# A two-layer state-space and attention kernel on one core: work moved across the seams between its stages

## The reference, cut to what matters

```
x = x + mixer(layernorm(x))        # state-space layer: 32 heads of 8 channels, 32 states
x = x + ffn0(layernorm(x))         # silu(w1 x) * (w2 x), gelu(h1 .), gelu(h2 .), w3
x = x + attention(layernorm(x))    # rms norm, 16 heads of 64, causal softmax, head gates, Wout
x = x + ffn1(layernorm(x))
```

## Time and profile before

| | |
|---|---|
| median of 3 runs | 1357.38 us (1356.96 to 1359.4) |
| profiled execution, own time | 1357.57 us |
| its span, first to last instruction | 1355.8 us |
| mean granted TensorE clock | 0.976 of full |
| busy: TensorE (PE) | 1277.2 us, 94% |
| busy: VectorE (DVE) | 908.5 us, 67% |
| busy: ScalarE (ACT) | 638.1 us, 47% |
| busy: GpSimd (POOL) | 588.2 us, 43% |
| moved by DMA | 143.51 MB, mean 106 GB/s |

### The profile page before, as it was taken

One profiled execution on the slowest core, in us unless ns is written; L12 is line 12 of the kernel. 1 busy time (PEld: TensorE's weight loads), 2 busy tenths in 40 slices (PEclk: granted clock), 3 DMA queues, 4 the chain that ended last, 5 costly groups with the idle time before them and its releaser, 6 DMA issues. The chain is left out here.

```text
span 1355.8 us, 22860 instructions
## 1 busy us (share of the span) xinstructions
PE 1277.2 (94%) x7798; PEld 709.1 (52%) x7798; DVE 908.5 (67%) x1773; ACT 638.1 (47%) x1537; POOL 588.2 (43%) x939
## 2 busy tenths in 40 slices
PE   7999677999999999998899998999999999899999
PEld 4443224566566566555445454555555556454545
DVE  6999996888988998989301206788787787530100
ACT  3266213555555565565322315566565665622221
POOL 2632315787888878888200002444344353410000
PEclk7999888999999999999899999999999999899999
DMA  2368896555555555556100002000000000000000
GB/s 81 155 256 339 317 391 218 192 183 183 187 188 184 183 185 190 185 183 235 63 0 0 0 1 88 1 1 1 1 1 1 1 1 1 1 1 0 16 0 15
DMA packets 67714, 143.51 MB, mean 106 GB/s; under 512 B 6800, under 2 KB 22800, under 8 KB 64784
## 3 DMA queue, kind: packets, MB, share of 16 engines
q1 hardware_dynamic: 62992, 129.47, 27.0%
q10 hardware_dynamic: 4608, 12.58, 2.3%
HBM read 94.58 MB, written 47.45 MB: 105 GB/s over the span
## 5 line engine op out<-in xcount | busy, mean ns | idle before, releaser
L1775 POOL TENSOR_SCALAR pr<-pr,rs,sg 128x512 f32<-128x512 f32 (+3 forms) x256 | 151.8, 607 | 209.4 <-DVE rs L1677 209.4
L615 PE MATMUL banks<-w_bc,valueT 128*128 128x512 f32 x448 | 212.0, 597 | 3.9 <-ACT own L909 3.1
L974 DVE TENSOR_TENSOR pp<-banks,rec 128x1024 f32<-128x1024 f32 x128 | 156.1, 1220 | 9.4 <-DMA dd<-det 3.3
L1588 ACT ACTIVATE pr<-banks,nm 128x512 f32<-128x512 f32 (+3 forms) x256 | 132.5, 523 | 24.9 <-DVE nm L1671 22.1
L615 PEld LDWEIGHTS banks<-w_bc,valueT 128*128 128x128 f32 x448 | 77.3, 192 | 61.4 <-issue 60.4
L1671 DVE TENSOR_REDUCE nm<-banks 128x2 f32<-128x1024 f32 (+3 forms) x128 | 105.5, 824 | 4.4
L1576 ACT COPY prT<-banks 128x512 f32<-128x512 f32 (+3 forms) x128 | 54.2, 424 | 112.0 <-PE banks L1472 111.8
L1056 POOL TENSOR_SCALAR_AFFINE_SELECT bp<-bp 128x1024 f32<-128x1024 f32 x64 | 73.5, 1148 | 76.4 <-ACT bp L863 76.3
L1312 DVE TENSOR_TENSOR x<-x,banks 128x256 f32<-128x256 f32 x16 | 6.7, 421 | 148.3 <-PE banks L1223 148.3
L856 ACT COPY qk<-banks 128x512 f32<-128x512 f32 x128 | 74.9, 585 | 64.2 <-PE banks L743 64.2
L1472 PE MATMUL banks<-ident,pr 128*128 128x128 f32 x640 | 98.7, 285 | 5.3 <-ACT prT L1576 4.1
(11 more groups left out here) (239 smaller groups left out, 2422.2 us busy)
## 6 DMA issues: line engine op xcount, KB each, us to landing
rec<-psi SPq DMA_DIRECT2D x128, 512.0 KB, 4.4
psi<-X SPq DMA_DIRECT2D x15, 2048.0 KB, 7.3
det<-w_bc ACTq DMA_DIRECT2D x16, 512.0 KB, 4.6
dd<-det SPq DMA_DIRECT2D x64, 128.0 KB, 4.7
bcs<-pre ACTq DMA_DIRECT2D x16, 256.0 KB, 6.8
w_bc<-in_w_bc SPq DMA_DIRECT2D x4, 1024.0 KB, 10.8
back<-bcs SPq DMA_DIRECT2D x16, 256.0 KB, 4.9
w_bc<-in_f_h SPq DMA_DIRECT2D x4, 1024.0 KB, 7.7
```

The lines of the kernel that those rows point to most:

```text
L615: mm = pe.matmul(bank, m["valueT"][:, c, t * P:(t + 1) * P], w, start=(c == 0), stop=(c == 1))
L974: dve.tensor_tensor(pp[:, q % 2].rearrange("p (a c) n -> p a c n", c=2), sc.unsqueeze(2).broadcast_to([P, 4, 2, HN]), rec[:, n % RL, q % 2 ...
L1588: act.activation(pr[:, n % RP, h, 0:w], S[n % 2][:, h, 0:w], ACT.Exp, bias=nm[:, n % 4, h:h + 1], accum_out=sm[:, m % 3, n % 2, h:h + 1]). ...
L1775: pool.tensor_scalar(row, row, rs[:, n // 2 % 2, n % 2, h:h + 1], sg[:, TPB * b + it, hd:hd + 1], ALU.mult, ALU.mult).then_inc(s["scaled"], 1)
```

## The change

Four things move, and nothing is computed otherwise but two roots.

- The expansions of `phi` and their copies to `ent`, `pick` and `own` go from the prologue of `mix` into `front`: TensorE expands right behind its four projections, with four banks in turn; `pick` and `pre` now lie in the buffer `xp`, free by then. `skip` is loaded in the front.
- In `mix` the first pair's records are loaded and awaited unit by unit, four loads instead of two, with semaphores `first`; `dd` has its own semaphores `dd_loaded`, for which POOL waits instead of DVE; `w_out` is loaded ahead of pair 2 and awaited by the first `project_out`; the clearing of `hz` comes after the first scale; TensorE runs four matmuls whose result nobody reads.
- At the attention's start q of group 0 and the first scores come ahead of the eight value chunks, which use the other four banks; k and q of group 1, gates and row transposes come with couple 1. ACT spreads its value copies around the first two exponentials.
- At the attention's end the projection of the last sequence is added up pair by pair over four banks: pairs 0 and 1 once the last exponentials have been taken, 2 to 4 and 5 and 6 between the last transposes and values, pair 7 at the end. Both roots become Ln and then Exp with factor -0.5.

```diff
 # front, TensorE, behind the four projections
+            pe.wait_ge(s["pick"], 2)
+            pe.wait_ge(s["phi"], 4)
+            pe.wait_ge(s["pre_taken"], len(PREPARED))
+            for n in range(LINKS // 2):
+                if n >= 4:
+                    pe.wait_ge(s["ent"], n - 3)
+                for q in range(2):
+                    for f in range(2):
+                        for i in range(4):
+                            mm = pe.matmul(k.bank[n % 4][32 * i:32 * i + 32, (2 * q + f) * P:(2 * q + f + 1) * P],
+                                           pick[:, f, LINKED[2 * n + q]],
+                                           phi[:, i // 2, :, (i % 2) * 2 * N:(i % 2 + 1) * 2 * N])
+                mm.then_inc(s["ent_ready"], 1)
 # front, ACT
+            act.wait_ge(s["skip_loaded"], 16)
+            for f in range(2):
+                act.mul(m["own"][:, f], k.ident[:], skip[:, f:f + 1]).then_inc(s["own"], 1)
...
+            for n in range(LINKS // 2):
+                act.wait_ge(s["ent_ready"], n + 1)
+                act.copy(m["ent"][:, 2 * n:2 * n + 2].rearrange("p t f c -> p (t f c)"), k.bank[n % 4][:]).then_inc(s["ent"], 1)
 # mix, SyncE
-            sp.dma_start(w_out[:], ins["w_out"].rearrange("(c p) d -> p c d", p=P)).then_inc(s["o_loaded"], 16)
-            sp.dma_start(skip[:], ins["skip"].rearrange("(c p) -> p c", p=P), allow_slow_non_contiguous=True).then_inc(s["o_loaded"], 16)
...
+                if n == 0:
+                    for u in range(2):
+                        sp.dma_start(rec[:, 0, u, 0:4].rearrange("p c n -> p (c n)"), span[0, :, u]).then_inc(first[u], 16)
+                        sp.dma_start(rec[:, 0, u, 4:8].rearrange("p c n -> p (c n)"), psi[0, 1:P + 1, u]).then_inc(first[u], 16)
...
+                sp.dma_start(dd[:, r], det[t, :, g]).then_inc(dd_loaded[r], 16)
 # mix, TensorE
-            for n in range(LINKS // 2):
-                if n >= 3:
-                    pe.wait_ge(s["ent"], n - 2)
-                expand(n)
-            pe.wait_ge(s["ent"], LINKS // 2)
-            pe.wait_ge(s["o_loaded"], 32)
-            pe.wait_ge(s["own"], 2)
+            for _ in range(4):
+                pe.matmul(SE[:], k.ident[:], m["valueT"][:, 0, 0:4 * P])
 # attention, TensorE
             project_k(0)
-            for j in range(2 * TPB):
...
             project_q(0)
-            pe.wait_ge(s["k_taken"], 1)
-            project_k(1)
-            pe.wait_ge(s["q_taken"], 1)
-            project_q(1)
-            pe.wait_ge(s["k_taken"], 2)
-            gates(0, OB)
...
                 if m == 0:
+                    for j in range(2 * TPB):
+                        if j >= 4:
+                            pe.wait_ge(s["v_taken"], j - 3)
+                        value_chunk(0, j, FIRST[j % 4][:])
+                if m == 1:
+                    pe.wait_ge(s["v_taken"], 2 * TPB - 1)
+                    project_k(1)
+                    pe.wait_ge(s["v_taken"], 2 * TPB)
+                    project_q(1)
+                    pe.wait_ge(s["k_taken"], 2)
+                    pe.wait_ge(s["q_taken"], 2)
+                    value_chunk(1, 0, PJ[:])
+                    gates(0, OB)
                     turn_rows(2)
                     turn_rows(3)
+                if m == COUPLES:
+                    pe.wait_ge(s["exped"], 4 * COUPLES)
+                if m >= COUPLES:
+                    for c in LAST_OUT[m - COUPLES]:
+                        add_pair(c)
...
-            for t in range(TPB):
-                project_out(B - 1, t, k.bank[t][:, 0:D])
+            add_pair(PAIRS - 1)
 # attention, new function
+            def add_pair(c):
+                pe.wait_ge(s["taken"], PAIRS * (B - 1) + c + 1)
+                for t in range(TPB):
+                    mm = pe.matmul(k.bank[t][:, 0:D], attT[:, (PAIRS * (B - 1) + c) % RA, t * P:(t + 1) * P], wo[:, c],
+                                   start=(c == 0), stop=(c == PAIRS - 1))
+                    if c == PAIRS - 1:
+                        mm.then_inc(s["o_ready"], 1)
 # attention, ACT, the late root
-                    act.activation(frstd[:], fvar[:], ACT.Sqrt, scale=1.0 / D, bias=eps[:, 0:1]).then_inc(s["fstd"], 1)
+                    act.activation(frstd[:], fvar[:], ACT.Ln, scale=1.0 / D, bias=eps[:, 0:1]).then_inc(s["fstd"], 1)
+                    act.wait_ge(s["fstd"], 1)
+                    act.activation(fvar[:], frstd[:], ACT.Exp, scale=-0.5).then_inc(s["frstd"], 1)
```

More of the change, by code:

```diff
@@ L37 @@
 NBLK = P // STEPS
+LINKED = [t for t in range(TILES) if t % TPB != TPB - 1]
+LINKS = len(LINKED)
 PREPARED = list(range(7, TILES * HG, HG))
@@ L663, in mix @@
         s = {n: sem("mx_" + n) for n in (
-            "own", "bcp", "eps", "mean", "var", "std", "rstd", "row",
+            "bcp", "eps", "mean", "var", "std", "rstd", "row",
             "o_loaded", "bc", "sq", "ss", "root", "rn", "scaled", "prod", "bt", "ca", "ct", "tp", "qk", "s",
             "pm", "masked", "uz", "hz_clear", "yg", "gs", "tk", "hT", "turned", "hz", "yg_done", "out", "oc", "x", "ygc",
-            "ent_ready", "ent", "pick")}
+            )}
         loaded = [sem(f"mx_tl{r}") for r in range(RL)]
+        first = [sem(f"mx_first{u}") for u in range(2)]
+        dd_loaded = [sem(f"mx_dd{r}") for r in range(RL)]
         back = sb("back", P, 2, 4 * HN)
@@ L1545, in _ @@
                     turn(2 * (m - LAG) + 1)
-                if not odd and b + 1 < B:
+                if m > 0 and not odd and b + 1 < B:
                     pe.wait_ge(s["q_taken"], g + 2)
@@ L1618, in _ @@
             take_k(0)
-            for j in range(TPB):
-                take_v(j, k.bank[j][:])
+            take_q(0)
+            act.preload_act_table_set("natural_log_exp_and_others")
             act.wait_ge(s["vare"], 1)
-            act.activation(std[:], std[:], ACT.Sqrt).then_inc(s["std"], 1)
-            for j in range(TPB, 2 * TPB):
-                take_v(j, k.bank[j % 4][:])
-            take_q(0)
+            act.activation(std[:], std[:], ACT.Ln).then_inc(s["std"], 1)
+            act.wait_ge(s["std"], 1)
+            act.activation(rstd[:], std[:], ACT.Exp, scale=-0.5).then_inc(s["rstd"], 1)
+            for j in range(2):
+                take_v(j, FIRST[j][:])
+            exponentials(0)
+            for j in range(2, 4):
+                take_v(j, FIRST[j][:])
+            exponentials(1)
+            for j in range(4, 2 * TPB):
+                take_v(j, FIRST[j % 4][:])
             take_k(1)
             take_q(1)
-            take_gates(0, OB)
             for m in range(COUPLES + LAG):
@@ L1735, in _ @@
                 if m == 0:
+                    dve.wait_ge(s["rstd"], 1)
+                    for n in range(HALF):
+                        dve.tensor_scalar(rows[:, HALF + n], k.x[:, HALF + n], mv[:, n, 0:1], rstd[:, n:n + 1], ALU.subtract,
+                                          ALU.mult).then_inc(s["row"], 1)
+                if m == 1:
+                    take_v(1, 0, PJ[:])
                     finish_gates(0)
```

101 lines of the change are left out of this document (41 added, 60 removed).

## The result

The changed kernel takes 1347.79 us in the median of 15 runs (1346.13 to 1357.92), the kernel before in the same job 1357.38 (1352.74 to 1361.08, 15 runs). The ratio is 0.9942, with a 95% interval from 0.9925 to 0.9959: 7.9 us less, between 5.6 and 10.2. The medians lie 9.6 us apart, the means 7.9 (1349.5 against 1357.4): eight of the changed kernel's 15 runs lie between 1346.1 and 1347.8, the other seven between 1348.4 and 1357.9. In a later job the changed kernel had 1350.32 (12 runs) against 1357.19, ratio 0.9944 (0.9923 to 0.9964).

The account below looks back on a forecast made before the run. TensorE, busy nearly throughout, bounds the kernel, leaving three seams: front to mixer, attention's start and its end. Gains of 1.9 + 1.3 + 4.7 = 7.9 us take the median from 1357.38 to 1349.5 us, range 1345.8 to 1354.5.

Parts of the forecast that it names:

- signs that I had named for being wrong: Half clock in the last couples or at the second FFN's start, or first product over 6 us behind the mixer's begin.
- Term 1: Front to mixer: the reduction of pair 2 starts at 224.4 instead of 226.32, 1.9 us sooner (-0.3 to 3.0).
- rival B: Front to mixer: transfers to the first product still take 7.2 us, making that gain -0.5: 1351.9 us; chance 0.15.
- rival E: Whole kernel: scarcely any change, from two clock falls, slow first transfers and POOL's 64 waits (3 us); chance 0.08.
- Term 2: Attention's start: stops of 2.9 us removed, new ones of 1.6 added, 1.3 us gained (0 to 2.9).
- Rival C: Attention's start gives nothing: 1350.8 us; counted with the forecast, no chance of its own.
- Term 3: Attention's end: 1.6 sooner start, 2.6 clock, 0.9 short stops, less 0.4 for additions: 4.7 us gained (2.1 to 5.6).
- Rival A: Attention's end or second FFN: the clock falls all the same; one fall gives 1352.1 us, two 1354.7; chance 0.17.
- Rival D: Attention: table loads come back at each of twelve tiles' moments, 31 us of ACT, 1380 us; chance 0.04.

Follow-up runs that it names:

- after: The first profiled execution of the changed kernel, nothing altered: 1347.47 us, span 1345.7 us.
- att_only: Front and mixer of the kernel before, with the attention of the changed kernel: 1353.37 us, ratio 0.9971.
- mix_only: Front and mixer of the changed kernel, with the attention of the kernel before: 1355.32 us, ratio 0.9993.
- sqrt_back: The changed kernel with the root of the attention's last rows as Sqrt and reciprocal again, pairwise projection kept: 1347.47 us, ratio 0.9946.
- out_whole: The changed kernel with the attention's last projection whole at the end again, Ln and Exp kept: 1352.42 us, ratio 0.9962.
- units_early: The changed kernel with the first four units projected one each behind the 11th to 14th prepared projection, not behind the 16th: 1350.25 us, ratio 0.9962.
- ring3: The changed kernel with three buffers instead of two for the prepared projections' way to memory: 1351.43 us, ratio 0.9953.

## Why the prediction was right, and where it was not

Forecast 1349.5 us, measured 1347.79 and 1350.32; 7.9 us less, measured 7.9 and 7.6 by the ratios. Most mechanisms were right; three sizes were off, and a gain and a loss were missed. That these errors cancel in the total is luck: by the terms, the first pair of profiles gained 10.1 us and the second 6.4. One of the signs that I had named for being wrong is met: half clock shows at the second FFN's start. And the first product, due not before 216, came at 215.89 in `after`, where the mixer began at 211.27 and not at 212.8. The lower end of the range, from terms of 3.0, 2.9 and 5.6, comes to 1345.9 and not 1345.8.

**Front to mixer (Term 1, 1.9 us).** The steps I can check: `pick`, the skip load and `own` cost nothing that shows; expansions at full clock 5.45 us, forecast 5.5; the mixer's begin to the first product 4.6, forecast 4.8; to pair 2's reduction 11.2, forecast 11.6; the projections' end to the begin 7.3, forecast 7.4. The profiled execution gained 3.9, since its projections ended right at phi, where I took 205.4. But the term hangs on that end, and I treated it as a fixed mark. With phi's place kept, the gain is (4.3 + 18.1) - (7.2 + 11.2) = 4.0 us, less what the projections end behind phi. The 18.1 and the 11.2 are not fixed either: the old way took 15.8 in `att_only`, which would make it 1.7 instead of 4.0, and the new one 12.3 in two executions. The middle of the nine executions with projections ahead of the expansions is 1.9 us behind (mix_only counted as 0.4), which leaves 2.1; in `sqrt_back` and `out_whole` the term is a loss of 1.4 and 3.2. That is what rival B was called, the front's tail eating term 1, though by another mechanism than the one I gave it: I had looked at the mixer's transfers, which took no part, and not at the stores at the front's end, for which ACT waits 42.7 us in all in the trace of before. What was shown is how the mixer's begin follows the projections' end; the copies that wait for stores are in the traces. What makes one execution's stores later than another's was not found: with three buffers the last copy came once at 184.3 and once at 202.4, and from 160 to 200 us the 16 DMA engines show a busy share of 98% in the one and 101% in the other.

**The parts of Term 1.** The four extra matmuls are worth 2.1 us of pair 2's reduction in one execution without them, where I gave up to 1.5; in two executions that have them (`sqrt_back`, `units_early`) the first projection ran at half clock all the same, and the reduction came 1.1 us later than in the other six. Loading the first records by unit is worth 0.4. The clearing of `hz` ahead of the first product costs 0.9 there, and is not saved by moving it on to the ninth product. POOL's wait for `dd`, 64 times, costs 0: the steady part is 591.18 and 591.06 us in the two executions without a fall there. With that rival E's estimate falls.

**The attention's start (Term 2, 1.3 us).** 21.8 to 20.4 is 1.4 in nine of the eleven executions with the new start; in two it is a loss of 0.3, since half clock comes at 834. The two new stops are 0.69 and 0.78 us, 1.5, where I had 1.6. Rival C is out. What I missed is in the middle: 1.5 us in every profile, and it is the clock. From the third couple's scores to the fifth's it is 11.15 us before (839.29 to 850.44) and 11.16 after (833.96 to 845.12); from there to the sixth's, 7.41 and 5.84. The fifth's and sixth's scores, first of the kernel before, then of the changed one:

```profile
850.44 1.55 PE L1463 MATMUL banks<-valueT,w_bc 64*128 64x512 f32 x8
857.85 1.35 PE L1463 MATMUL banks<-valueT,w_bc 64*128 64x384 f32 x8
...
845.12 1.35 PE L1472 MATMUL banks<-valueT,w_bc 64*128 64x512 f32 x8
850.96 1.35 PE L1472 MATMUL banks<-valueT,w_bc 64*128 64x384 f32 x8
```

All three executions with the old start have a stretch at half clock between 848 and 857, none with the new start has. That the new order of gates and chunks is what takes it away fits all fourteen, but no run takes the order apart.

**The attention's end (Term 3, 4.7 us).** 4.9 us in the first pair of profiles, 2.3 in the second. The difference is the clock of the kernel before: half clock behind the stand of 2.8 us in one execution, none behind the same stand in the other. So the 2.6 us that I put down as removed are saved only in executions that have them; the lower end of the term, 2.1, was the better figure for the second profile. The rest, by `out_whole` and the second profile of before, is 1.4 for the projection by pairs (forecast 0.9 less 0.4) and 21.6 - 20.7 = 0.9 for the root (forecast 1.6). The exponentials did come 1.2 us sooner behind their maxima; TensorE waited 1.62 us ahead of the first pairs, not 1.1. The last addition ends 16.6 us behind the start of the copy behind the last exponentials, forecast 17.3: the four additions come out in 0.96 us, so I had overpriced them.

**Rival A, the clock.** Not in the last couples, but at the other place I had named, the stand ahead of the second FFN: 1.7 us in both profiles of the changed kernel, and in four of the five others that have its attention's end unchanged (`units_early` has none). So the rival that I gave 0.17 came in part, as one fall, priced at 2.6 us and measured at 1.7, and the sum held because gains that I had not counted paid for it. In `sqrt_back` the clock fell ahead of the last transposes and then not at the FFN; whether that is why its measured time did not go up by the 2.4 us that its end takes longer is not shown. The fall may also account for the halves: the profiles of `mix_only` and `att_only` each have the 1.7 us that the whole change has once, so 0.9 + 3.9 + 1.7 = 6.5 us. That is an estimate from one profile of each, and noise alone would do too. The Trainium skill, page TensorE: Matmul & The Clock Gate, section Part 1, has half clock as the state without activity. `ring3` agrees where the stand is 16.2 us: the expansions ran at 0.50. For stands of one to three us it decides nothing here, as the two profiles of before show.

**Rival D**: refuted. No table load stands among the moments of the twelve tiles, nor ahead of the Ln at 1164.17. The table switch costs what the earlier trace rows say, one load of 1.28 us, here again in `sqrt_back` (1173.80, the exponential at 1175.10). The Trainium skill's 2.66 us for a switch (page ScalarE: Activation LUTs, section What ACT_TABLE_LOAD costs) would have made the root worth more than the 0.9 us of the traces.

**Open.** `out_whole` should by its trace be level with the changed kernel (1.4 us more at the end, 1.7 less in the FFN); its ratio of 0.9962 is 2.4 to 2.7 us worse, with intervals that overlap (0.9949 to 0.9975 against 0.9923 to 0.9964). One profile does not say which of its executions have the fall. By the ratios nothing that ran beats the changed kernel.

## What to carry to other kernels

A mark that lies under cover can move about unseen; work hung behind it inherits its spread, so look at what ends just ahead of the wait that is removed, and take a second profile before trusting any gain of a few us. At a seam the clock belongs to the price of an order: with TensorE busy just ahead of the work that matters, that work came out shorter here (by 2.1 us behind the four extra matmuls in one pair of profiles, by 1.8 to 2.8 for expansions right behind projections). That pays only where TensorE would stand anyway, since the same matmuls at the attention's end cost 1.3 of the 1.7 us that they saved. Parts that are measured alone need not add up to the whole, since each can pay a cost that the whole pays once; here that is a possible reading and not shown.

## What the runs showed of the hardware

- At the second FFN's start a fall of the granted clock comes whole or not at all: that FFN takes 157.4 to 157.5 or 159.1 to 159.2 us in fourteen executions, never a time between.
- The same stop of TensorE, 2.80 and 2.81 us in two executions of one program, is followed by half clock in one and full clock in the other.
- Expansions (192 matmuls of 128 columns) take 5.45 us behind projections at full clock, 8.09 and 8.27 after a stand of 16.2 and 6.6 us.
- The stores of the projections made ahead, 256 KB each, land 2.3 to 14.4 us after their issue in one execution (`after`), while the scan's records are being stored.
